# Edge aggregation of a graph kernel: 128-row tiles with full-array products, against 64-row halves in quadrants of TensorE

## What is computed

```
xn  = layernorm(x)
agg = segment_sum(edge_weight[:, None] * xn[src], dst)           # 212500 rows of 256
gnn = relu(((1 + eps) * xn + agg) @ W1.T + b1) @ W2.T + b2
mix = hyperbolic linear attention of xn: qkv, batch norm, depthwise and pointwise conv,
      relu'd linear attention, output projection
x   = x + gnn + mix
out = x + scatter(w_sel * (gelu(layernorm(x)[sel] @ w1 + b1) @ w2 + b2))   # sel: the top 6249 of 12500 rows
```

## Time and profile before

| what | value |
|---|---|
| median of 3 runs | 2598.59 us (2598.03 to 2598.87) |
| profiled execution: time, span | 2601.07 us, 2599.4 us |
| mean granted TensorE clock | 0.988 |
| busy: PE, PE weight loads, DVE, ACT, POOL | 2475.5, 2169.1, 1804.0, 1461.6, 1769.9 us |
| DMA | 192007 packets, 333.45 MB, mean 128 GB/s |

### The profile page before, as it was taken

The page is one execution under the profiler, slowest core; times in us unless marked ns, Lnnn a source line. Parts: engine busy times, 40 slices in busy tenths (PEclk is TensorE's granted clock), DMA queues, the critical chain, the costliest instruction groups (busy, mean ns, idle before and its releaser), DMA issues.

```text
span 2599.4 us, 42294 instructions
## 1 busy us (share of the span) xinstructions
PE 2475.5 (95%) x12654; PEld 2169.1 (83%) x12654; DVE 1804.0 (69%) x5986; ACT 1461.6 (56%) x3513; POOL 1769.9 (68%) x1879
## 2 busy tenths in 40 slices
PE   4898999999999999999999999999999999999996
PEld 3677888887888888888888888888788888888786
DVE  6847676676766768667667776675866767767557
ACT  3755565565655656556565565665655656556431
POOL 2037777777777777777777777777777777777500
PEclk9899999999999999999999999999999999999998
DMA  7643444434444344443444434444344343343338
GB/s 231 189 132 107 128 115 120 125 114 129 115 121 126 114 120 123 121 124 116 120 125 116 130 115 120 124 117 128 113 120 123 115 130 116 115 124 114 97 117 282
DMA packets 192007, 333.45 MB, mean 128 GB/s; under 512 B 46287, under 2 KB 133965, under 8 KB 191673
## 3 DMA queue, kind: packets, MB, share of 16 engines
q0 software_dynamic: 86752, 238.17, 32.0%
q1 hardware_dynamic: 105018, 92.42, 11.1%
HBM read 291.99 MB, written 38.46 MB: 127 GB/s over the span
## 4 chain that ended last, share of the span: by engine, by line
PE 78%; DVE 9%; DMA 5%; ACT 5%; issue 1%; SPq 0%; POOL 0%; DVEq 0%; POOLq 0%
PE bank L1157 23%; PE qkv L1252 13%; PE bank L1264 12%; PE bank L1171 9%; PE bank L1201 6%; DMA work<-in_x 5%; PE qkv L1181 4%; PE bank L498 2%; PE qkv L1180 2%; DVE rings L960 2%; PE bank L1217 2%; PE bank L1226 2%; PE bank L1191 2%; ACT work L796 1%; ACT work L799 1%
## 5 line engine op out<-in xcount | busy, mean ns | idle before, releaser
L766 POOL DMA_INDIRECT rings<-xn_dram,window x1764 | 1744.0, 989 | 615.9 <-issue 388.4
L1157 PE MATMUL bank<-rings 128*128 128x256 f32 x3528 | 885.3, 381 | 17.9 <-DVE rings L960 14.3
L1157 PEld LDWEIGHTS bank<-rings 128*128 128x128 f32 x3528 | 657.4, 191 | 111.1 <-DVE rings L960 25.6
L960 DVE TENSOR_SCALAR rings<-iota,window_dst,window 128x128 f32<-128x128 f32 x1764 | 559.9, 363 | 139.2 <-PE bank L1157 125.6
L1252 PE MATMUL qkv<-work,ffn_weights 128*128 128x256 f32 x1568 | 365.4, 381 | 0.0
L1264 PE MATMUL bank<-ffn_weights,work 128*128 128x256 f32 x1568 | 362.0, 379 | 0.0
L856 ACT ACTIVATE work<-qkv,fb 128x256 f32<-128x256 f32 x392 | 159.8, 472 | 312.8 <-PE qkv L1252 312.3
L1264 PEld LDWEIGHTS bank<-ffn_weights,work 128*128 128x128 f32 x1568 | 297.2, 190 | 40.0
L1252 PEld LDWEIGHTS qkv<-work,ffn_weights 128*128 128x128 f32 x1568 | 295.7, 191 | 38.5
L1171 PE MATMUL bank<-resident,weights 128*128 128x256 f32 x1176 | 277.8, 379 | 0.0
L1171 PEld LDWEIGHTS bank<-resident,weights 128*128 128x128 f32 x1176 | 223.3, 190 | 30.3
(11 more groups left out here) (240 smaller groups left out, 3364.6 us busy)
## 6 DMA issues: line engine op xcount, KB each, us to landing
rings<-xn_dram,window POOLq DMA_INDIRECT x1764, 2.8
xn_dram<-work SPq DMA_DIRECT2D x14, 896.0 KB, 7.7
work<-xn_dram SPq DMA_DIRECT2D x49, 256.0 KB
work<-in_x SPq DMA_DIRECT2D x48, 256.0 KB
out<-work SPq DMA_DIRECT2D x48, 256.0 KB
work<-in_x SPq DMA_DIRECT2D x9, 896.0 KB, 5.7
rings<-out SPq DMA_DIRECT2D x6, 896.0 KB, 8.6
out<-rings SPq DMA_DIRECT2D x6, 896.0 KB, 6.3
```

Source lines behind the costliest of these rows:

```text
L766: nc.gpsimd.indirect_dma_start(out=msg[q][:, :], out_offset=None, in_=xn_dram[:, :], in_offset=bass.IndirectOffsetOnAxis(ap=window[t % WIN ...
L960: v.tensor_scalar(sel[k % SEL_RING], iota[:, :], window_dst[b][:, k % SLOTS:k % SLOTS + 1], window[b][:, k % SLOTS, 2:3].bitcast(F32), ALU ...
L1157: te.matmul(agg[h][:, 0:D], sel[k % SEL_RING], msg[q], start=first, stop=last, skip_group_check=True).then_inc(slot_used, 1)
```

## The change

The edges are kept by 64 rows of nodes instead of 128. A slot still holds 128 gathered edges, but its upper and lower 64 partitions hold edges of different halves of the tile. In even slots partitions 0 to 63 hold edges of half 0 and 64 to 127 of half 1, in odd slots the other way round. Each slot becomes two products of a 64x64 one-hot with 64x256 rows, in two quadrants of TensorE; an even and an odd slot together use all four. Even slots accumulate into banks[3], odd ones into banks[4], the two tiles of a step side by side in the columns of both; `take_sup` adds both banks in two instructions. One-hots are 64 wide, with a ring of 18. A half has 18 x 64 = 1152 places. Slots are multiplied in bursts of six at positions 5, 11, 17, 23, 29 and 35. The first slot of the second tile now waits until the first tile's sup is taken. The bounds need four thresholds a tile instead of two, window loads are four transfers a tile instead of one, a remainder chunk loads its edges in two transfers, and the blocks of a step have new positions. `bn_moments` comes ahead of the first two h1 blocks.

```diff
-SEL_RING = 12
+SEL_RING = 18
+HALF = 64
+BURST = 6
-    WIN = SLOTS * P
+    PAIRS = SLOTS // 2
+    WIN = SLOTS * HALF
...
         def tables_bounds(pool):
             pool.wait_ge(border_ready, 1)
-            for k in range(2):
+            for k in range(4):
                 nc.gpsimd.indirect_dma_start(
...
+        def tables_halves(dve):
+            v = nc.vector
+            for n in range(2):
+                for r in range(2):
+                    v.tensor_copy(at_half[n][HALF * r:HALF * (r + 1), :],
+                                  iota[HALF * r:HALF * (r + 1), HALF * (n ^ r):HALF * (n ^ r) + HALF])
+            for r in range(2):
+                rows_ = slice(HALF * r, HALF * (r + 1))
+                v.memset(own_half[rows_, HALF * (1 - r):HALF * (1 - r) + HALF], -BIG)
+                v.tensor_copy(own_half[rows_, HALF * r:HALF * (r + 1)], iota[rows_, HALF * r:HALF * (r + 1)])
+            link = Link(dve, bounds_link, 6, 1)
+            link(v.tensor_scalar(thr_half[:NT, 0:1], thr[:NT], float(HALF), None, ALU.add))
+            link(v.tensor_scalar(tmp_p[:NT], ends_bc[:NT, 0, :], thr_half[:NT, 0:1], BIG, ALU.is_lt, ALU.mult))
+            link(v.tensor_tensor(tmp_p[:NT], tmp_p[:NT], iota_m[:NT], ALU.add))
+            v.tensor_reduce(lohi[:NT, 1:2], tmp_p[:NT], AX_X, ALU.min)
+            link(v.tensor_scalar(thr_half[:NT, 1:2], thr[:NT], float(HALF - 1), None, ALU.add))
+            link(v.tensor_scalar(tmp_p[:NT], ends_bc[:NT, 1, :], thr_half[:NT, 1:2], None, ALU.is_le))
+            link(v.scalar_tensor_tensor(tmp_p[:NT], iota_m[:NT], 1.0, tmp_p[:NT], ALU.add, ALU.mult))
+            v.tensor_reduce(lohi[:NT, 2:3], tmp_p[:NT], AX_X, ALU.max).then_inc(bounds_link, 1)
+            link.close()
...
                 if g == 2:
                     tables_chunks(dve)
+                if g == 3:
+                    tables_halves(dve)
                 if g == 4:
                     tables_borders(dve)
...
-        PE_AT = dict(sup=0, x3=0, qkv=(0, 10), w1=1, h1=(12, 17, 20), w2=4, outT=(13, 23), ft=(16, 27), hid=(23, 23,
-                     27, 29), y=(31, 32, 32, 35))
-        DVE_AT = dict(scale=(5, 10), out=(6, 13), c=(12, 18), ft=(14, 29), sup=(27, 0), n4=1, f=4, y=5, x=3,
-                      combine=(6, 12), rstd=16, tail_out=(20, 24), stage=(0, 27))
+        PE_AT = dict(sup=2, x3=0, qkv=(2, 12), w1=3, h1=(12, 19, 22), w2=8, outT=(14, 25), ft=(21, 33), hid=(23, 26,
+                     26, 28), y=(29, 32, 32, 35))
+        DVE_AT = dict(scale=(3, 9), out=(6, 13), c=(12, 17), ft=(14, 30), sup=(13, 0), n4=0, f=3, y=1, x=5,
+                      combine=(6, 12), rstd=16, tail_out=(21, 27), stage=(2, 27))
...
         def load_window(eng, t):
-            first = eng.value_load(bounds[0:1, 2 * t:2 * t + 1], min_val=0, max_val=ET * P)
-            after(eng, slot_used, RING + (t - WINDOWS + 1) * SLOTS)
-            eng.dma_start(window[t % WINDOWS][:, :, :].rearrange("p k c -> p (k c)"),
-                          edges[bass.ds(first * 3, 3 * WIN)].rearrange("(p n) -> p n", p=P)
-                          ).then_inc(window_landed[t % WINDOWS], 16)
+            flat_window = window[t % WINDOWS][:, :, :].rearrange("p k c -> p (k c)")
+            for u in range(2):
+                first = eng.value_load(bounds[0:1, 3 * t + u:3 * t + u + 1], min_val=0, max_val=ET * P)
+                if u == 0:
+                    after(eng, slot_used, RING + (t - WINDOWS + 1) * SLOTS)
+                for n in range(2):
+                    r = u ^ n
+                    eng.dma_start(flat_window[HALF * r:HALF * (r + 1), 3 * PAIRS * n:3 * PAIRS * (n + 1)],
+                                  edges[bass.ds((first + HALF * PAIRS * n) * 3, 3 * HALF * PAIRS)].rearrange("(p n) -> p n", p=HALF)
+                                  ).then_inc(window_landed[t % WINDOWS], 16)
...
             def rem_chunk(t):
                 counted(pool, rem_used, rem)
...
+                for u in range(2):
+                    at_ = pool.snap(rem_at[u], min_val=0, max_val=3 * (ET * P + WIN))
+                    pool.dma_start(rem_edges[HALF * u:HALF * (u + 1), :],
+                                   edges[bass.ds(at_, 3 * HALF)].rearrange("(p n) -> p n", p=HALF)
+                                   ).then_inc(rem_edges_landed, 16)
+                    pool.reg_add(rem_at[u], rem_at[u], 3 * HALF)
...
-                v.tensor_scalar(sel[k % SEL_RING], iota[:, :], window_dst[b][:, k % SLOTS:k % SLOTS + 1],
-                                window[b][:, k % SLOTS, 2:3].bitcast(F32), ALU.is_equal, ALU.mult
+                c = column(k % SLOTS)
+                v.tensor_scalar(sel[k % SEL_RING], at_half[k % 2], window_dst[b][:, c:c + 1],
+                                window[b][:, c, 2:3].bitcast(F32), ALU.is_equal, ALU.mult
                                 ).then_inc(sel_ready, 1)
...
-                v.scalar_tensor_tensor(sup[h], xnin[h], eps1_col, agg[h][:, 0:D], ALU.mult, ALU.add
-                                       ).then_inc(sup_ready, 1)
+                link(v.scalar_tensor_tensor(sup[h], xnin[h], eps1_col, agg[0][:, h * D:(h + 1) * D], ALU.mult, ALU.add))
+                v.tensor_tensor(sup[h], sup[h], agg[1][:, h * D:(h + 1) * D], ALU.add).then_inc(sup_ready, 1)
...
+            def quadrants(h, n, one_hot, rows_, start, stop):
+                for r in range(2):
+                    u = n ^ r
+                    ins = te.matmul(agg[n][HALF * u:HALF * (u + 1), h * D:(h + 1) * D], one_hot[HALF * r:HALF * (r + 1)],
+                                    rows_[HALF * r:HALF * (r + 1)], start=start, stop=stop, skip_group_check=True,
+                                    tile_position=(HALF * r, HALF * u))
+                return ins
...
-            def edge(i, k):
-                h, q = k // SLOTS, k % RING
-                first, last = k % SLOTS == 0, k % SLOTS == SLOTS - 1
-                if first:
-                    after(pe, sup_ready, i * 2 + (h - 1))
-                if last:
-                    remainder(i, h)
-                pe.wait_ge(sel_ready, i * STEP_SLOTS + (k + 1))
-                pe.wait_ge(msg_landed[q], i * (16 * TURNS) + 16 * (k // RING + 1))
-                te.matmul(agg[h][:, 0:D], sel[k % SEL_RING], msg[q], start=first, stop=last,
-                          skip_group_check=True).then_inc(slot_used, 1)
+            def edges_of(i, first):
+                for k in range(first, first + BURST):
+                    h, q = k // SLOTS, k % RING
+                    start, stop = k % SLOTS < 2, k % SLOTS >= SLOTS - 2
+                    if k % SLOTS == 0:
+                        after(pe, sup_ready, i * 2 + h)
+                    if k % SLOTS == SLOTS - 2:
+                        remainder(i, h)
+                    pe.wait_ge(sel_ready, i * STEP_SLOTS + (k + 1))
+                    pe.wait_ge(msg_landed[q], i * (16 * TURNS) + 16 * (k // RING + 1))
+                    ins = quadrants(h, k % 2, sel[k % SEL_RING], msg[q], start, stop)
+                    if k % 2:
+                        ins.then_inc(slot_used, 2)
...
                 for k in range(STEP_SLOTS):
-                    if i > 0 or k >= EARLY_EDGES:
-                        edge(i, k)
+                    if k % BURST == BURST - 1 and (i > 0 or k >= EARLY_EDGES):
+                        edges_of(i, k - (BURST - 1))
```

139 lines of the change are left out of this document (74 added, 65 removed).

## The result

The changed kernel takes 2683.34 us in the median of 4 runs (2680.58 to 2686.16), the kernel before beside it 2598.31: **1.032 of it, 95% interval 1.0307 to 1.0333**. That is 85 us more, where 38 was forecast (2637). The profiled execution has a span of 2680.1 us against 2599.4, so there are 80.7 us to place.

What follows compares the result with a forecast made beforehand. The prediction took GpSimd's gathers and TensorE to bound the kernel at nearly one pace. Terms of +15, -4, +39 and -12 us summed to +38 us, 2637 us on the median, with a range of 2600 to 2715 us.

Steps and rivals of the forecast that it cites:

- the five terms: Whole kernel: loop start +15, GpSimd's waits -4, remainder chunks +39, loop end -12 us; mean gather time unchanged.
- POOL sets the pace: Main case for the loop: GpSimd's gathers, 1.296 us each, bound the changed kernel; 2615 to 2660 us, chance 0.58.
- the one-hots shrink, the others stay, so the mean of a gather stays: Gathers on GpSimd: 1764 as before, with VectorE's longer instructions unchanged, so still 1.296 us each including the gap.
- Remainders: Between tiles on GpSimd: six remainder chunks run for the first time, uncovered, 39 us in all (26 to 57).
- The start: Before the loop: doubled threshold tables and more border gathers shift everything by 15 us (11 to 17).
- The end: After the last gather's start: TensorE's lag shrinks, its last burst ending 7.5 us later instead of 19.6, -12 us.
- POOL's waits: Over the loop: the some 4 us that GpSimd waited beyond its fixed gap may go, -4 us.
- The pair of slots: Edge products on TensorE: two slots in four quadrants take 0.55 us, between ends of 0.43 and 1.73; 9.9 us a step.
- A change of mode: TensorE between quadrants and full array: each of 12 changes a step exposes 0.163 us, 2.0 us a step.
- In order: Rival on TensorE: records start strictly in program order, so two slots still cost 0.86 us; 2710 us, chance 0.17.
- Quicker gathers: Rival on GpSimd: less contention with VectorE frees up to 79 us of gather time, giving 2558 us; chance 0.14.
- TensorE's relief: TensorE's need in an FFN step falls from 47.2 to 43.5 us, under GpSimd's 46.7; only its lag reaches the end.

## Why the prediction was wrong in size

The direction, the bound and four of the five terms hold; the fifth, the gathers' mean, is what was forecast at nothing.

- **The pace.** "POOL sets the pace" holds: PE waits 103.7 us for transfers, as was forecast (100 and more), and the gathers stand 0.30 us apart. That the kernel before has two engines at nearly one pace is borne out by the run with every other gather, 2603 us, with the comparison across chips that it needs.
- **The step that failed** is "the one-hots shrink, the others stay, so the mean of a gather stays". The mean went from 0.989 to 1.015 us: +46.7 us where the sum had 0. The rows had the mechanism, but I read it from the wrong line: L980 begins at 201.20, 0.55 us into the gather at 200.65, and such an operation costs nothing. The one that counts is the one ahead of it, under way at 200.65 with 0.52 us left, which gives 0.39 of the gather's 1.34 us:

```profile
200.43 0.74 DVE L979 SCALAR_TENSOR_TENSOR work<-work 128x512 f32<-128x512 f32 x1
```

So I took the excess as a constant of the DVE work, and it hangs on where each operation stands when a gather starts: 242 gathers were lengthened before, 358 after. I moved every block of the step and treated that as nothing. As the cover had been declared gone ("POOL has no slack"), a price that hangs on where two engines meet needed a range. With the measured excess my sum gives 38 + 47 = 85. That 85 is also the difference of the medians is in part luck: the sum was made for the profiled execution, where 80.7 were measured, and the other 4 us are the remainders' 39 for 35.0.
- **Remainders**: +39 forecast, +35.0 by the trace and 33.4 by their removal. The count of six was right; the wait for landing was 2.18 us where I took 3.0.
- **The start**: +15 forecast, +14.2 measured, and the first gather at 180.7 where about 182 was said. The parts are less exact: VectorE's wait for the border rows grew from 7.59 to 8.43 us, not by the 2.7 of two more gathers, and the small copies took 1.5 us for 1.0.
- **The end**: -12 forecast, -12.3. The last burst ends 7.1 us after the last gather's start, forecast 7.5. **POOL's waits**: -4 forecast, -3.
- **The pair of slots**: 0.55 us taken, 0.432 measured, which is the best end. The weight loads, that made me stay away from it, bound nothing. **A change of mode**: 0.163 us taken, 0.09 measured at either side of a burst. Both were hidden, so neither moved the sum.
- **In order** (0.17, 2710 us) fell. Its time was nearer to the result than mine, but by another mechanism: a pair takes 0.43 us and not 0.86. I had it that the two records of one product must both be out before the next product's first. By the records, the first records of the four products start together, and the four second records 0.216 us after them. The Trainium skill's rule ("TensorE: Matmul & The Clock Gate", Part 3) is not contradicted by that, only the time that I worked out from it.
- **Quicker gathers** went the other way: the contention that it names is the term that decided, with the opposite sign. With it at 0.14 and "the mean stays" in every other case, no case of mine had slower gathers.
- **TensorE's relief**: I had 43.5 us of need in an FFN step; the records' counts give 40.8. With POOL's pace gone the step still takes 45.1 us, from the chain of ACT and DVE. I had called the blocks' new waits "within PE's slack". With POOL setting the pace that held.

## What to carry to other kernels

When two engines stand at one pace, as here, relief of one was worth nothing but the 12 us at the end, and every cost on the other was paid in full: ask first for the time with either one's work thinned out. A duration whose mean lies above its median can be a meeting of two engines; if a change moves blocks, that difference is an unknown with a range, not a constant. Look for VectorE operations with two SBUF inputs that are under way when a GpSimd gather starts: here five of them a half were worth 92 us, once POOL alone set the pace.

## What the runs showed that I had not expected

- fp32 products, two records each, run fully beside each other in four quadrants: 24 records of a burst in 1.53 us.
- An indirect gather on GpSimd costs by the instruction: 0.907 us for 64 rows, 0.946 for 128, and 0.30 us of gap for both.
- A gather that starts under a DVE operation on two SBUF inputs is longer by what is left of it less 0.13 us (581 of 585 gathers in the two kernels). An operation on PSUM and SBUF costs it nothing, nor does one that begins 0.40 us into the gather, nor L985, which begins 0.03 to 0.05 us before it; and the operation that begins inside a gather is not held up by it.
- Some chips run these kernels 15 to 20% slower with all gathers. On the one of them where half the gathers were left out, the kernel before took 2603 us. In their traces an engine starts microseconds after the work that it waits for; why is open.
